# State-space stage of a decoder: the step-size products and ScalarE's softplus steps issued one state earlier

## The reference

```
xs = silu(conv4(x @ in_w_x) + conv_b)            # 4 taps, causal
dt, B, C = split(xs @ xproj_w)                   # 8, 16, 16 columns
dt = softplus(dt @ dt_w + dt_b)                  # step size, one per channel and row
h[t] = exp(dt[t] * A[d,s]) * h[t-1] + dt[t] * B[t,s] * xs[t]
y[t] = sum over s of h[t,d,s] * C[t,s]  +  D * xs[t]
out = (y * silu(z)) @ out_w
```

## Time and profile before

| | us |
|---|---|
| median of 3 runs (lowest, highest) | 7300.41 (7296.68, 7302.1) |
| the profiled execution: its own time | 7294.51 |
| its span, first to last instruction | 7292.4 |
| busy in the span: PE / DVE / ACT / POOL | 6507.4 / 5360.5 / 4055.2 / 2820.5 |
| state-space stage, start of its first scan and of its last | 2287.3 and 4156.6 |

### The profile page before, as it was taken

The page is one execution under the profiler, slowest core; times in us unless marked ns, Lnnn a source line. Parts: engine busy times, 40 slices in busy tenths (PEclk is TensorE's granted clock), DMA queues, the critical chain, the costliest instruction groups (busy, mean ns, idle before and its releaser), DMA issues. The chain is left out here.

```text
span 7292.4 us, 189527 instructions
## 1 busy us (share of the span) xinstructions
PE 6507.4 (89%) x74836; PEld 3973.7 (54%) x74836; DVE 5360.5 (74%) x8933; ACT 4055.2 (56%) x6024; POOL 2820.5 (39%) x1680
## 2 busy tenths in 40 slices
PE   7989987887697989989999779989899999989998
PEld 5767665444442333333333356666576767667676
DVE  7877576665556999999999856677577777768544
ACT  3556343665446777777777745455344444456433
POOL 3321175332214888888888601165021212211000
PEclk9999978999888999999999989999999999999999
DMA  1000000000001222222222100000000000000000
GB/s 29 0 21 13 3 11 8 3 3 2 14 2 52 76 73 75 75 80 77 76 75 76 51 12 13 9 31 3 12 2 2 2 2 2 2 15 14 2 0 23
DMA packets 115881, 190.04 MB, mean 26 GB/s; under 512 B 38661, under 2 KB 74746, under 8 KB 114970
## 3 DMA queue, kind: packets, MB, share of 16 engines
q1 hardware_dynamic: 112218, 183.47, 7.9%
q10 hardware_dynamic: 3264, 0.54, 0.1%
HBM read 173.87 MB, written 7.98 MB: 25 GB/s over the span
## 5 line engine op out<-in xcount | busy, mean ns | idle before, releaser
L2600 POOL TENSOR_TENSOR m_dBx<-m_dtx,m_Bs 128x1024 f32<-128x1024 f32 x515 | 1165.8, 2283 | 227.3 <-DVE m_hs L2965 185.2
L2965 DVE TENSOR_TENSOR_SCAN m_hs<-m_ps_dA,m_dBx 128x512 f32<-128x512 f32 x1030 | 1200.5, 1207 | 56.4 <-POOL m_dBx L2600 55.8
L2719 PE MATMUL m_ps_y<-m_yc,ident 128*128 128x512 f32 x2060 | 1021.6, 619 | 0.0
L2824 ACT ACTIVATE m_ps_dA<-m_dt,m_A 128x504 f32<-128x504 f32 x1030 | 682.0, 678 | 427.1 <-DVE m_hs L2965 424.4
L2096 POOL TENSOR_TENSOR a_s<-a_s,a_den 128x1024 f32<-128x1024 f32 x128 | 243.5, 1902 | 1123.9 <-DVE a_den L2142 1123.9
L2976 DVE TENSOR_TENSOR m_yc<-m_hs,m_ps_C 128x1024 f32<-128x1024 f32 x515 | 616.3, 1197 | 1.3 <-PE m_ps_C L2700 1.3
L2719 PEld LDWEIGHTS m_ps_y<-m_yc,ident 128*128 128x128 f32 x2060 | 350.5, 190 | 357.0 <-issue 357.0
L2700 PE MATMUL m_ps_C<-m_parts,m_sel 48*128 48x512 bf16 x516 | 199.8, 387 | 175.7 <-DVE m_yc L2976 175.6
L2700 PEld LDWEIGHTS m_ps_C<-m_parts,m_sel 48*128 48x128 bf16 x516 | 47.7, 92 | 566.9 <-DVE m_yc L2976 421.2
L625 POOL TENSOR_TENSOR c_kbd<-c_kf,c_hmask 128x1024 f32<-128x1024 f32 x66 | 125.0, 1893 | 515.9 <-ACT c_kf L534 492.0
L2140 DVE TENSOR_REDUCE a_den<-a_s 128x16 f32<-128x1024 f32 x128 | 156.0, 1219 | 207.0 <-ACT a_s L2047 207.0
(11 more groups left out here) (748 smaller groups left out, 16025.2 us busy)
## 6 DMA issues: line engine op xcount, KB each, us to landing
m_Bs<-BC_rows SPq DMA_DIRECT2D x258, 512.0 KB, 3.5
c_kvb<-in_ctxT SPq DMA_DIRECT2D x68, 128.0 KB, 2.1
c_kvb<-in_ctxT SPq DMA_DIRECT2D x17, 256.0 KB, 2.7
out_dram<-X SPq DMA_DIRECT2D x1, 4096.0 KB
BC_rows<-m_low SPq DMA_DIRECT2D x33, 64.0 KB, 2.7
part_rows<-m_split SPq DMA_DIRECT2D x33, 48.0 KB, 1.7
m_parts<-part_rows SPq DMA_DIRECT2D x33, 48.0 KB, 1.7
m_piece<-BC_rows SPq DMA_DIRECT2D x33, 32.0 KB, 1.7
```

The source lines that it names most:

```text
L2600: return nc.gpsimd.tensor_tensor(to, one, other, ALU.mult)
L2719: last = nc.tensor.matmul(ps_y[:, m, :], C.ident[:], of[:, m, :], start=s == 0, stop=s == NS - 1)
L2824: nc.scalar.activation(seqs(ps_dA[:, h % 3, :]), seqs(dt[:, par, m, :]), ACT.Exp, scale=A[:, second, m, s:s + 1]).then_inc(decay, 1)
L2965: nc.vector.tensor_tensor_scan(hs[:, s % HS, m, :], ps_dA[:, (2 * s + m) % 3, :], dBx[:, s % BX, m, :], 0.0, ALU.mult, ALU.add).then_inc(s ...
```

## The change

Five constants change in the two functions front: TensorE's step_sizes goes from state 4 to state 3, and ScalarE's four steps go from states 7, 8, 9 and 10 to 6, 7, 8 and 9. GpSimd's front keeps its states 11 to 15, and no wait is added or taken away.

```diff
@@ TensorE, front
-                elif s == 4:
+                elif s == 3:
                     step_sizes(j, in_loop)
@@ ScalarE, front
-                elif s == 7:
+                elif s == 6:
                     act.wait_ge(dt_done, j + 1)
...
-                elif s == 8:
+                elif s == 7:
                     act.drain()
...
-                elif s == 9:
+                elif s == 8:
                     act.drain()
...
-                elif s == 10:
+                elif s == 9:
                     act.drain()
```

## The result

| | before | after |
|---|---|---|
| median of the runs made side by side, 4 each | 7301.26 us | 7422.57 us |
| lowest, highest | 7296.68, 7308.97 | 7415.27, 7426.12 |
| the profiled execution: its own time, its span | 7294.51, 7292.4 | 7415.27, 7413.2 |
| first scan of the stage to its last | 2287.3 to 4156.6 | 2288.4 to 4279.1 |

The ratio is 1.0164, with a 95 % interval of 1.0151 to 1.0177: the change makes the kernel 1.6 % slower, by 121 us. The stage itself grows from 1869.3 to 1990.7 us, by 121.4, so all of it lies there.

A forecast was written before the change was run, and what follows sets the result against it. VectorE was taken as the bound. 30 groups at 4.4 - 0.74 = 3.66 us give 110, two at the turn 9, together 119 on 7294.5: 7413.5, forecast as 7420 us against the median; range 7335 to 7440.

The forecast's parts named there:

- GpSimd's pause goes: At L2620: the logarithm ends 3.36 us earlier, so GpSimd no longer stands still from 3011.14 to 3014.19.
- TensorE's products at state 3: Step-size products behind the add of state 2: cost 0, at worst 0.1 in each of 32 groups, 3 us.
- The cost at split_rows, 4.4: VectorE's split_rows meets a busy GpSimd, so the scan of state 9 starts 4.4 us later in each group.
- the second of my two cases: At split_rows: the cast waits for GpSimd too, and the scan of state 9 starts 4.55 us later.
- The middle: At split_rows: 4.4 us, taken between 4.3 if the cast passes freely and 4.55 if it waits.
- The bound: At split_rows: it can't get worse, as GpSimd's state 13 product needs the scan behind; the fourth instruction finds GpSimd waiting.
- The gain at the group's end, 0.74 of 1.22: The scan's stall of 1.22 goes, but late TensorE holds the gain to 0.74 us a group, 22 us in 30.
- the stall: At the group's end: VectorE's scan waits 1.22 us for GpSimd's product of the next group's state 0.
- TensorE's pause, 0 and at worst 6 us: TensorE pauses about 5 us behind state 8, then runs slower: 0, at worst 0.2 a group, 6 us.
- The sum: Over the stage: 110 us for 30 groups with the stall plus 9 for two at the turn, 119 us.
- The rival without a collision: At split_rows: subtractions slip past GpSimd or GpSimd waits; 7278 us, or 7263 if TensorE is not late; 9%.
- half a collision: At split_rows: two close subtractions pass one boundary with a free cast, scan 2.0 late; 42 us, 7342; 13%.

The follow-up runs named there:

- e2: The kernel after the change with only ScalarE's last two steps put back to states 9 and 10: 7304.21 us, ratio 1.0001.
- e1: The kernel after the change with one wait added, GpSimd's first chain step L2620 also waiting for split_rows to end: 7303.74 us, ratio 0.9998.
- e4: The kernel after the change with one more subtraction in split_rows, into a spare tile nobody reads: 7422.81 us, ratio 1.0159.
- e7: e5 with TensorE's convolutions at states 11, 13 and 14 and ScalarE's copy of their rows at state 12: 7285.51 us, ratio 0.9978.
- e3: The kernel before the change with only split_rows one state later, behind the weighting of state 8: 7438.74 us, ratio 1.0185.
- e5: The kernel after the change, split_rows moved between state 6's scan halves, behind the weighting of state 5, drawn ahead: 7304.81 us, ratio 1.0008.
- e6: The kernel before the change with the same move of split_rows as e5 and nothing else: 7334.69 us, ratio 1.0048.

## Why the prediction was right

*GpSimd's pause goes.* As forecast: L2620 starts without a wait, right behind its product, at 3056.37. e2 shows that the logarithm alone decides this. That GpSimd worked "without a stop" before was not exact: it had short gaps with no visible reason, such as the 0.39 in the earlier trace rows; no term of the sum hangs on them.

*TensorE's products at state 3 cost nothing.* Nearly as forecast: e1 and e2 keep them there, and both measure as the kernel before. What I did not see coming is the add behind them. Before the change and in e1 it takes 1.98 in all 32 groups; after the change 2.57 to 3.60 in 14 of them, and in three of these the weighting of state 5 waits, 0.95 us in all, within the 3 us that I had allowed. The longest:

```profile
3239.35 3.60 PE L2719 MATMUL m_ps_y<-m_yc,ident 128*128 128x512 f32 x4
...
3243.44 1.22 DVE L2976 TENSOR_TENSOR m_yc<-m_hs,m_ps_C 128x1024 f32<-128x1024 f32 x1 [0.41 <-PE m_ps_C L2700]
```

*The cost at split_rows, 4.4.* Measured 5.28 - 0.89 = 4.39. I had left open whether the cast passes; it waits, 0.45 us instead of 0.19, so the second of my two cases holds. That one I had put at 4.55: neighbouring GpSimd instructions overlap by about 0.05 in the rows, so the boundaries come a little earlier than the sum of the durations. The middle was right because two small things cancel, which is luck. The Trainium skill (SBUF — State Buffer, Who interferes with whom) has it that a cast can need the shared port as well and that whoever starts first holds it for a whole instruction; both agree with these rows. The bound, that GpSimd runs dry behind two more instructions, is shown by the idle 2.86 and by e4.

*The gain at the group's end, 0.74 of 1.22.* In a group in which TensorE is on time, the interval grows by 3.62, so the gain is 4.39 - 3.62 = 0.77. I had expected all the lateness at L3002, at 0.66; it shows 0.42 in the group looked at, and a mean of 14.3 / 32 = 0.45. The rest goes in small steps ahead of it. The weighting of state 15 and the scan behind it, before:

```profile
3041.04 1.20 DVE L2976 TENSOR_TENSOR m_yc<-m_hs,m_ps_C 128x1024 f32<-128x1024 f32 x1
3042.15 2.33 DVE L2965 TENSOR_TENSOR_SCAN m_hs<-m_ps_dA,m_dBx 128x512 f32<-128x512 f32 x2
```

And after, from the scan ahead of them to L3002:

```profile
3087.15 2.33 DVE L2965 TENSOR_TENSOR_SCAN m_hs<-m_ps_dA,m_dBx 128x512 f32<-128x512 f32 x2
3089.58 1.22 DVE L2976 TENSOR_TENSOR m_yc<-m_hs,m_ps_C 128x1024 f32<-128x1024 f32 x1
3090.86 2.34 DVE L2965 TENSOR_TENSOR_SCAN m_hs<-m_ps_dA,m_dBx 128x512 f32<-128x512 f32 x2
...
3093.62 1.22 DVE L3002 TENSOR_TENSOR m_e<-m_sz,m_ps_y 128x1024 f32<-128x1024 f32 x1 [0.42 <-PE m_ps_y L2719]
```

From the scan to the weighting it is 2.43, against 3041.04 - 3038.78 = 2.26 before, and from there to the next scan 1.28 against 1.11: 0.17 lost at each, and 0.42 - 0.22 = 0.20 at L3002, together 0.54. A scan that does not wait starts 0.09 before the weighting ahead of it has ended in the rows, so the stall had cost 1.31 and not 1.22; 1.31 - 0.54 is the 0.77. That TensorE's convolutions are the cause at L3002 is borne out by e7.

*TensorE's pause, 0 and at worst 6 us.* It stands still for 5.17 and runs at 0.50 of its clock behind that. In most groups it has idle time again before its convolutions, as at 3077.20, and nothing is lost. In eight groups it has none to be seen, and in five of these the weighting of state 15 waits 0.17 to 0.48 for it, together 1.5 us: so much the pause can have cost in them. The others of the 13 waits, 4.9 us in all, are the three behind the step-size products (0.95), three at the convolutions of the turn (1.5, against 0.7 before), one in the first group (0.22) and one in the last (0.64, the same before).

*The sum.* 110 for the 30 groups with the stall is 107.4 + 3.6 = 111.0 in the trace; 9 for the two at the turn is 5.78 + 4.27 = 10.1. The first of these two grows by more than the collision because the weighting waits 1.9 us for TensorE in it, against 0.7 before. Forecast 119 of the profiled execution and 7420 us; measured 121 and 7422.57. The rival without a collision falls by the durations of the subtractions; half a collision falls because the two that stand close together are let in at one boundary each.

## What to carry to other kernels

Before moving work earlier on one engine, look at what the engines beside it do in the time that this fills: a pause can be what keeps two instructions apart, and short ones with two SBUF inputs on VectorE, 0.22 us each here, cost 2.2 to 2.4 us each, one GpSimd instruction, for as long as GpSimd had work. Durations that never vary in a trace prove nothing about an overlap that never happens in it; look for another line of the same kind that does meet it. If a pause goes, move the short work out of its place in the same edit, and check what the new place holds back.

## What the runs showed that was not expected

A cast of 128 x 64 elements, with one SBUF input, is held by GpSimd like the subtractions: 0.45 us after the change and up to 1.64 us in e3, against 0.184 when GpSimd stands still. GpSimd pays next to nothing for it: its product takes 2.28 to 2.31 us in the group shown, against 2.28 and 2.29 before.

TensorE's clock fell in e5 behind step-size products of 8 rows, without any pause ahead of them in the rows from 2987 on: 0.76 was granted from 2996 to 3003, and the add took 3.68. One group later, in the same order of work, it took 1.98. The place of the products does not decide it alone: in e6, whose TensorE has the order of the kernel before, the add behind them takes 2.60 to 3.68 in 12 of the 32 groups, and in the kernel before 1.98 in all of them. I had taken a slower clock to need a pause such as the one in the earlier trace rows, and that was wrong. What picks the groups stays open.
